# Layer 0's edge loop: one-hots and attention product on GpSimd, weighting and gating in one operation each, the step's order changed

## The reference

```
msg = (s_n @ W_src)[src] + (s_n @ W_dst)[dst]          # likewise the vectors
m1_s, m1_v = _cg_tp(msg_s, msg_v, y0, y1, w1...)        # first product, w1 = rbf @ W_rbf
a = (m1_s @ W_alpha).reshape(e, 4, 16)
a = where(a > 0, a, 0.2 * a)                            # leaky
a = sum(a * alpha_dot, axis=-1)                         # the attention product: 4 logits per edge
amax = segment_max(a, dst);  ex = exp(a - amax[dst])
val_v = (m1_v @ Wv_val) * sigmoid(val_s @ Wg)           # gated; val_s = m1_s @ Ws_val
m2_s, m2_v = _cg_tp(sigmoid(val_s), val_v, y0, y1, ...) # second product
h = concat(m2_s @ Ws_vlin, m2_v @ Wv_vlin)              # 4 heads x 40
agg = segment_sum(ex * h, dst) / segment_sum(ex, dst)   # values weighted
```

## Time and profile before

| | before |
|---|---|
| time, median of 3 runs | 12605.16 us (12595.29 to 12611.27) |
| the profiled execution | 12581.97 us, its span 12580.2 us |
| granted TensorE clock, mean | 0.852 of full speed |
| busy: PE, DVE, ACT, POOL | 10064.0, 9184.8, 7070.5, 6371.8 us (80, 73, 56, 51% of the span) |

### The profile page before, as it was taken

One profiled execution on the slowest core, in us unless ns is written; L12 is line 12 of the kernel. 1 busy time (PEld: TensorE's weight loads), 2 busy tenths in 40 slices (PEclk: granted clock), 3 DMA queues, 4 the chain that ended last, 5 costly groups with the idle time before them and its releaser, 6 DMA issues. The chain is left out here.

```text
span 12580.2 us, 245481 instructions
## 1 busy us (share of the span) xinstructions
PE 10064.0 (80%) x46500; PEld 7042.4 (56%) x46501; DVE 9184.8 (73%) x32444; ACT 7070.5 (56%) x26255; POOL 6371.8 (51%) x9502
## 2 busy tenths in 40 slices
PE   4421389999999999999998888888788888888887
PEld 2211277777777777777777544445433335544445
DVE  6720188888888888888887699995455564699996
ACT  0000166666666666666665455654466665576774
POOL 0677555555555555555542255552255552355552
PEclk9855588888888888888887799997799997799997
DMA  6433211111111111111111233333122223233333
GB/s 252 56 65 72 55 30 28 29 28 29 29 28 29 29 28 28 29 28 29 27 16 18 70 87 85 88 87 53 40 51 52 52 53 43 69 87 86 87 87 61
DMA packets 1798442, 691.93 MB, mean 55 GB/s; under 512 B 1586190, under 2 KB 1677258, under 8 KB 1798346
## 3 DMA queue, kind: packets, MB, share of 16 engines
q0 software_dynamic: 219136, 411.56, 13.7%
q1 hardware_dynamic: 1572154, 275.26, 12.9%
q10 hardware_dynamic: 7056, 4.02, 0.1%
HBM read 514.24 MB, written 171.77 MB: 55 GB/s over the span
## 5 line engine op out<-in xcount | busy, mean ns | idle before, releaser
L961 POOL DMA_INDIRECT shared<-table,rec x2640 | 2562.8, 971 | 2674.1 <-issue 1040.8
L1043 PE MATMUL bank<-tp,oh 128*128 128x480 f32 (+1 forms) x5280 | 2405.9, 551 | 6.6 <-DVE tp L1120 3.6
L995 ACT ACTIVATE tp<-tp,rec 128x64 f32<-128x64 f32 x7920 | 2030.2, 335 | 211.4 <-DVE tp L1091 132.7
L1035 PE MATMUL bank<-w_fc,hT 128*128 128x448 f32 x2640 | 1367.6, 600 | 685.1 <-ACT hT L979 444.8
L1675 ACT ACTIVATE shared<-bank 128x512 f32<-128x512 f32 x1760 | 1003.2, 596 | 1286.3 <-PE bank L1750 1208.5
L1750 PE MATMUL bank<-ident,tp 128*128 128x128 f32 x7040 | 1271.2, 341 | 294.4 <-ACT tp L811 293.7
L1043 PEld LDWEIGHTS bank<-tp,oh 128*128 128x128 f32 x5280 | 922.0, 195 | 855.8 <-issue 842.0
L1750 PEld LDWEIGHTS bank<-ident,tp 128*128 128x128 f32 x7040 | 1116.0, 183 | 340.5 <-ACT tp L811 330.7
L1091 DVE TENSOR_TENSOR tp<-bank,shared 128x256 f32<-128x256 f32 x1320 | 560.0, 424 | 907.7 <-PE bank L1043 616.1
L780 POOL DMA_INDIRECT rec_dst<-ACC x784 | 812.8, 1037 | 591.3 <-issue 561.1
L1639 POOL DMA_INDIRECT gat<-table,rec x880 | 867.2, 985 | 283.6 <-issue 176.8
(11 more groups left out here) (242 smaller groups left out, 23271.0 us busy)
## 6 DMA issues: line engine op xcount, KB each, us to landing
shared<-table,rec POOLq DMA_INDIRECT x2640
rec_dst<-tp SPq DMA_DIRECT2D x44, 900.0 KB, 23.2
ACC<-in_attrs SPq DMA_DIRECT2D x56, 623.0 KB
rec_src<-tp SPq DMA_DIRECT2D x44, 730.0 KB, 19.8
efr<-rec_src SPq DMA_DIRECT2D x440, 64.0 KB
efr<-rec_dst SPq DMA_DIRECT2D x440, 64.0 KB
ACC<-in_attrs SPq DMA_DIRECT2D x196, 130.0 KB
rec<-rec_dst SPq DMA_DIRECT2D x1320, 10.0 KB
```

The source lines that it names most:

```text
L961: nc.gpsimd.indirect_dma_start(out=gatx[:, u, g, 0:L.row], out_offset=None, in_=tables[L.n][:, :], in_offset=IOff(ap=rec[:, u, g, L.idx:L. ...
L995: done = nc.scalar.activation(t[:, g, lo:lo + 64], t[:, g, 0:64], ACT.Copy, scale=rec[:, u, g, L.y + k:L.y + k + 1])
L1035: nc.tensor.matmul(pW[u % 2][:, 0:448], hT[:, u % 2, :], fc2[:, :], start=True, stop=True)\
L1043: done = nc.tensor.matmul(pS[u % 2][:, 0:TW], oh[:, u, g, :], tp[:, u % 2, g, 64:64 + TW], start=g == 0, stop=g == G - 1)
```

## The change

All of it is in layer 0's loop. Nothing else of the program changes.

- `one_hot(a)` goes from VectorE to GpSimd, where it stands first in the step, ahead of GpSimd's part of the first product and of the gathers.
- The product of `la` with alpha_dot goes from VectorE to GpSimd (`along_dot`), between the gathers and GpSimd's part of the second product. VectorE's `logits` is split: `bend` (la) before the gates, the reduction after `keep`.
- `gates` is one operation on both groups. `weigh` is one operation: `pH` has 41 columns per head, the last one set to 1.0 once, so the operation writes 41 columns and the copy of `pex` is gone.
- The copy of the new maximum into `M` (`held`) goes from the head of the step to behind `weigh`.
- The block number of e is taken from the step before where that step is of the same loop iteration; its register load is gone in three of four steps.

```diff
-            pH, pG, pS = BK[7][:, 0:320], BK[7][:, 320:328], BK[7][:, 328:492]
+            pH, pG, pS = BK[7][:, 0:328], BK[7][:, 328:336], BK[7][:, 336:500]
...
+                    def one_hot(i, u):
+                        s4 = u % 4
+                        po.wait_ge(rec_in[s4].h, rec_in[s4].at(i * 32 + 32))
+                        po.sem_inc(pool_tick, 1)
+                        po.wait_ge(summed.h, summed.free(i, u, 4))
+                        po.sem_inc(pool_tick, 1)
+                        for g in range(G):
+                            last = nc.gpsimd.tensor_scalar(oh[:, s4, g, :], iota1[:, :], rec[:, s4, g, 0:1], None,
+                                                           ALU.is_equal)
+                        last.then_inc(oh_ready.h, 1)
+
+                    def along_dot(i, u):
+                        po.wait_ge(leak.h, leak.done(i, u))
...
+                        nc.gpsimd.tensor_tensor(la2[:, :, :], la[:, :, :],
+                                                W["ad"][:, :].unsqueeze(1).to_broadcast([P, G, 64]), ALU.mult)\
+                            .then_inc(dotted.h, 1)
...
+                        if a:
+                            one_hot(*a)
                         if b:
                             part(*b, msg[:, b[1] % 2], msg_ready, tp1_ready, 0, pooled1)
                         if a:
                             gather(*a)
                         if c:
+                            along_dot(*c)
                             part(*c, vsv[:, c[1] % 2], gated, tp2_ready, 1, pooled2)
...
+                nc.vector.memset(pH, 1.0).then_inc(zeroed_acc.h, 1)
...
+                        ve.wait_ge(squashed.h, squashed.done(i, u))
+                        nc.vector.tensor_tensor(
+                            vsv[:, u % 2, :, 64:160].rearrange("p g (i c) -> p g i c", i=3),
+                            pVv[:, :, 160:256].rearrange("p g (i c) -> p g i c", i=3),
+                            th2[:, :, 64:96].unsqueeze(2).to_broadcast([P, G, 3, 32]), ALU.mult)\
+                            .then_inc(gated.h, 1)
...
+                        last = nc.vector.tensor_tensor(
+                            hw[:, s2].rearrange("p g (h f) -> p g h f", h=4),
+                            pH.rearrange("p (g h f) -> p g h f", g=G, h=4),
+                            pex[:, s2].unsqueeze(3).to_broadcast([P, G, 4, 41]), ALU.mult)
...
                         if e:
-                            block_e = block_of(ve, *e)
+                            block_e = last_block[0] if last_block else block_of(ve, *e)
+                        last_block[:] = [block_d] if d and d[1] % 4 else []
...
                         if c:
-                            logits(*c)
+                            bend(*c)
                             gates(*c)
                         if e:
                             keep(*e, block_e, d)
+                        if c:
+                            logits(*c)
                         if d:
                             weigh(*d)
+                            held(*d, block_d)
```

More of the change, by code:

```diff
@@ L1527, in layer0_edges @@
             gated = sig4("gated_e", 1, NP)
-            leak = sig4("leak", 3, NP)
+            leak = sig4("leak", 1, NP)
+            dotted = sig4("dotted", 1, NP)
+            logit_ready = sig4("logit_ready", 1, NP)
             xm_ready = sig4("xm_ready", 1, NP)
@@ L1850, in distances, with bend, logits @@
                                                 ALU.subtract).then_inc(dlt_ready.h, 1)
-                    def logits(i, u):
+                    def bend(i, u):
                         ve.wait_ge(squashed.h, squashed.done(i, u))
+                        ve.wait_ge(dotted.h, dotted.free(i, u, 1))
                         nc.vector.tensor_tensor(la[:, :, :], pVv[:, :, 0:64], lk[:, :, :], ALU.max)\
                             .then_inc(leak.h, 1)
-                        ve.wait_ge(leak.h, leak.done(i, u, 1))
-                        nc.vector.tensor_tensor(la2[:, :, :], la[:, :, :],
-                                                W["ad"][:, :].unsqueeze(1).to_broadcast([P, G, 64]), ALU.mult)\
-                            .then_inc(leak.h, 1)
-                        ve.wait_ge(leak.h, leak.done(i, u, 2))
+                    def logits(i, u):
+                        ve.wait_ge(dotted.h, dotted.done(i, u))
                         nc.vector.reduce_sum(a4[:, u % 2], la2[:, :, :].rearrange("p g (h d) -> p g h d", h=4), AX.X)\
-                            .then_inc(leak.h, 1)
+                            .then_inc(logit_ready.h, 1)
                     def gates(i, u):
-                        for g in range(G):
-                            last = nc.vector.tensor_tensor(
-                                vsv[:, u % 2, g, 64:160].rearrange("p (i c) -> p i c", i=3),
-                                pVv[:, g, 160:256].rearrange("p (i c) -> p i c", i=3),
-                                th2[:, g, 64:96].unsqueeze(1).to_broadcast([P, 3, 32]), ALU.mult)
-                        last.then_inc(gated.h, 1)
+                        ve.wait_ge(squashed.h, squashed.done(i, u))
[4 more added lines that the diff above has]
+                            .then_inc(gated.h, 1)
                     def spread(i, u):
                         ve.wait_ge(xm0_ready.h, xm0_ready.done(i, u))
-                        ve.wait_ge(leak.h, leak.done(i, u, 3))
+                        ve.wait_ge(logit_ready.h, logit_ready.done(i, u))
                         ve.wait_ge(xm_t.h, xm_t.free(i, u, 1))
@@ L1896, in maxima, with held @@
                             .then_inc(mnew_ready.h, 1)
+                    def held(i, u, block):
                         ve.wait_ge(mnew_ready.h, mnew_ready.done(i, u))
                         ve.sem_inc(ve_tick, 1)
-                        nc.vector.tensor_copy(mrow, mnew[:, u % 2, :])
-                    def one_hot(i, u):
-                        s4 = u % 4
-                        ve.wait_ge(rec_in[s4].h, rec_in[s4].at(i * 32 + 32))
-                        ve.wait_ge(summed.h, summed.free(i, u, 4))
-                        for g in range(G):
-                            last = nc.vector.tensor_scalar(oh[:, s4, g, :], iota1[:, :], rec[:, s4, g, 0:1], None,
-                                                           ALU.is_equal)
-                        last.then_inc(oh_ready.h, 1)
+                        nc.vector.tensor_copy(flat(M[:, block, :]), mnew[:, u % 2, :])
                     def keep(i, u, block, d):
@@ L1932, in weigh @@
                         ve.wait_ge(summed.h, summed.free(i, u))
-                        for g in range(G):
-                            hv = hw[:, s2, g, :].rearrange("p (h f) -> p h f", h=4)
-                            nc.vector.tensor_tensor(
-                                hv[:, :, 0:40], pHv[:, g, :].rearrange("p (h f) -> p h f", h=4),
-                                pex[:, s2, g, :].unsqueeze(2).to_broadcast([P, 4, 40]), ALU.mult)
-                        last = nc.vector.tensor_copy(
-                            hw[:, s2].rearrange("p g (h f) -> p g h f", h=4)[:, :, :, 40], pex[:, s2])
+                        last = nc.vector.tensor_tensor(
+                            hw[:, s2].rearrange("p g (h f) -> p g h f", h=4),
+                            pH.rearrange("p (g h f) -> p g h f", g=G, h=4),
+                            pex[:, s2].unsqueeze(3).to_broadcast([P, G, 4, 41]), ALU.mult)
                         last.then_inc(hw_ready.h, 1)
@@ L1980, in step @@
                             spread(*c)
+                    last_block = []
                     pipeline(ve, step)
```

11 lines of the change are left out of this document (6 added, 5 removed).

## The result

The changed kernel is slower: 12772.58 us, median of 4 runs (12767.16 to 12796.06), against 12608.22 for the kernel before on the same chip. The ratio is 1.0132, 95% interval [1.0114, 1.0151], 164 us. The forecast was 12578 in a range of 12370 to 12700. The profiled execution has a span of 12763.9 us.

The account below looks back on a forecast made before the run. TensorE was taken to bound low-clock steps and VectorE full-clock ones; 0.78 us per four steps, cut to 0.25 by GpSimd's hits, is 0.06 a step, 27 us: 12605 - 27 = 12578 us, range 12370 to 12700.

Parts of the forecast that it names:

- The bound on either engine: Layer 0's loop: TensorE bounds low-clock steps, with no idle time before X; VectorE bounds full-clock steps, by 0.34 us.
- VectorE's 0.49 us: Middle of VectorE's step: alpha_dot product moved, gates and weighting merged, less the copy's 0.1; 0.49 us less in every step.
- What GpSimd's new work costs: GpSimd's step: one-hots at 0.7 us the pair delay its first-product part onto L833 and L834; net gain 0.06 us a step.
- rival of a late GpSimd: GpSimd's step: long one-hots push its first-product part into L833 and L834 every step; slower, put at 12680 us, chance 0.20.
- fewer falls: TensorE's clock in the loop: fewer pauses spare one low stretch in four, 0.28 us a step, 12457 or 12430; chance 0.20.
- The rhythm holds: Loop's four-step period, 47.78 us: steps are locked to the clock's changes, time stays 12605 us; chance 0.15.
- The head of the step: Start of VectorE's step: moving one-hots, copy and block load gains 0.05 us in full-clock steps, nothing in low-clock ones.

Follow-up runs that it names:

- e8: e1 plus four transposes of the identity on TensorE ahead of T1; ratio 0.9539 to the kernel before, step 10.65 us.
- e2: The kernel before with the one-hots alone moved to GpSimd, first in its step; ratio 1.0291 to the kernel before, step 12.65 us.
- e6: The changed kernel plus four transposes of the identity on TensorE ahead of T1; ratio 0.9820 to the kernel before, step 11.41 us.
- e1: The changed kernel with the one-hots alone put back on VectorE; ratio 0.9993 to the kernel before, step 11.96 us.
- e10: e1 plus four transposes of the identity between V and X instead of ahead of T1; ratio 1.0062 to the kernel before, step 12.24 us.
- e5: The changed kernel with both one-hots and the alpha_dot product back on VectorE; ratio 0.9938 to the kernel before, step 11.76 us.
- e4: The changed kernel with GpSimd's part of the first product left out, one-hots still on GpSimd; ratio 0.9702 to the kernel before, step 11.11 us.
- e7: The kernel before plus three transposes of the identity on TensorE ahead of T1; ratio 0.9911 to the kernel before, step 11.71 us.
- e3: The changed kernel with GpSimd's one-hots behind its part of the first product instead of ahead; ratio 0.9951 to the kernel before, step 11.87 us.
- e13: e6 with the copy of the maximum back behind mdiff; ratio 0.9781 to the kernel before, step 11.42 us.

## Why the prediction was wrong, point by point

**In short.** The loop was to gain 0.06 us a step and lost 0.44. The bound on either engine and VectorE's 0.49 us were read rightly. What failed is the step "What GpSimd's new work costs": it had the one-hot too short, followed the delay on GpSimd only to L833 and L834, and left the time at the lower clock as it was.

**The one-hot on GpSimd** is the term that failed first: 0.35 us taken, 0.612 measured, the pair 1.21 instead of 0.7. It was nearer to the upper bound (0.65). The ratio of 1.96 in the Trainium skill ("GPSIMD Engine Reference", Performance versus the Vector engine), from which the prediction estimated 0.64, agrees with the trace, where 612 against 325 ns is 1.88. The rival of a late GpSimd had this price and its mechanism, hits on L833 and L834, in it, and gave 12655 to 12658 (the case as a whole was put at 12680); the result is 115 us above that too. So two more terms were missing.

**GpSimd late a second time.** The prediction had the product with alpha_dot start 0.34 behind la, and a copy that costs 0.1 (bounds 0 and 0.17). In fact GpSimd comes from the gathers 0.50 behind la, the reduction waits 0.14, and the copy takes 0.73 in the step shown and 0.450 on average. The middle of VectorE's step, from la to the end of `spread`, was to be 0.49 shorter. It took 5.23 us before (3578.45 to 3583.68), takes 5.14 in the changed kernel (3113.06 to 3118.20), and 4.71 in e8, where la is at 2789.53 and `spread` ends at 2794.24. The 0.49 was well worked out (0.52 in e8); 0.43 of it is taken back by lateness on GpSimd that no term followed past the first product. The working did name the lock by which an operation waits for a whole one of GpSimd's (the Trainium skill, "SBUF — State Buffer", Who interferes with whom), and set it at 0.155 a hit. For L833 and L834 on msg that is about right (0.09 and 0.13 on average). The copy in the step shown was held for 0.57 us, nearly both operations of GpSimd's pair (0.65), which is more like the Trainium skill's rule, though for two operations and not one.

**The clock.** Of the two rivals on the clock one had fewer falls, the other an unchanged time. There was none in which a later T1 means more time at the low level. T1's pause went from 0.66 to 1.02 us a step and low time from 28 to 34% of the loop. The eight single steps show its size: the step of 15.95 us has the clock low through V, X, S and T2 on top of the usual places, and its set is 50.88 - 48.14 = 2.74 us longer than the other. That is 0.34 of the 0.43 us a step; the rest, 48.14 against 47.78 in four steps, is 0.09. It is an account of the rhythm, not a clean division into clock and direct cost: which direct delay brings the clock to fall there is not separable in these runs. They pull both ways. In e2 the hits are 0.16 us (0.25 with the waiting ahead of them) and the loss 0.71; but with the pause filled (e6 against e8) the one-hots on GpSimd cost 0.76 us a step, 0.67 of it plain delay on VectorE between two full-clock steps, more than the whole loss here. So how much of the loss is the clock's stays open. Shown is that more than the loss can be bought back by filling the pause (e6, -0.98 us a step), and, in e1, not by the same work elsewhere (e10).

**"The rhythm holds"**, at 0.15, described e1 exactly: without the one-hots on GpSimd the shorter step of VectorE was worth nothing. But the lock is not general: e5, with less moved, came out of it.

**What was right.** The head of the step is worth nothing: from message to dlt 2.85 against 2.89 us, and VectorE's wait for mg stands bare in every step (at 1.19 us longer than the 0.5 to 0.9 foreseen). oT does not wait for the one-hots in the changed kernel. L834 on msg is longer than 288 ns. There is no new wait before the message. Not so with X: they were to stand behind V without a gap, and do in most steps, but in 59 of 161 TensorE still waits 0.26 us ahead of them (V over at 3094.04, X at 3094.32, after the end of `spread` at 3094.27).

**Open.** The pause alone does not order the kernels: e4 and e1 have the same one (0.78) with a clock of 0.92 and 0.85, and e7 with 0.31 has less clock than e8 with 0.32; e3 has 0.49 and the clock of before. Where in the step the pause falls against the changes of the clock must matter as well, and no run here controls that.

## What to carry to other kernels

An operation moved to an idle engine is to be followed to the end of that engine's step: what stands behind it there comes late, and then meets other work (here 1.2 us of one-hots pushed two unrelated groups of GpSimd's operations onto operations that VectorE's step hangs on; behind the first group they cost nothing). Where TensorE bounds a loop and its granted clock is under 1, look for the pause before its clock falls: a few empty transposes in it were worth more (4.5%, e8 against e1) than everything taken off VectorE. And a period that stays the same to 0.01 us when work is removed is not set by that work.

## What the runs showed of the hardware that was not expected

- GpSimd's compare of a 128x128 one-hot takes 612 ns, VectorE's 325 ns.
- A copy of 4 columns on VectorE took 0.73 us where it started 0.06 us ahead of GpSimd's pair of t_dot, ending 0.02 us after it, and 0.16 us where it started 0.08 us ahead (steps of e3, e4 and e8; there L834 and L836 behind it take 0.44 and 0.43 us instead of 0.28). An operation on 64 columns took 0.78 instead of 0.21 us at the copy's place (e13).
- Two kernels with different work per step (VectorE busy 10.1 and 9.3 us) had the same 477.87 and 477.88 us in 40 steps, with the same time at the lower level, spread in different ways.
- Four transposes more per step made the loop 576 us shorter (e1 to e8) ahead of T1 and 123 us longer (e1 to e10) between V and X.
